# Stage 4 of a decoder kernel: the order of one pair's work on TensorE, and score matmuls of 512 columns

## The reference

```python
q = x @ Wq                                    # x: 32 x 64 x 128
xc = jnp.concatenate((mem, x), axis=1)        # mem: the context, so 128 keys
k, v = jnp.split(xc @ Wkv, 2, axis=-1)        # 16 heads of depth 8
dots = jnp.einsum('bhid,bhjd->bhij', q, k) * scale
dots = jnp.where(j_idx > i_idx + mem_len, -jnp.inf, dots)   # causal over the own tokens
attn = jax.nn.softmax(dots, axis=-1)
out = jnp.einsum('bhij,bhjd->bhid', attn, v).transpose(0, 2, 1, 3).reshape(b, n, dim)
return out @ Wout + bout                      # then x = layernorm(x + out)
```

## Time and profile before

| | before |
|---|---|
| median of 3 runs | 856.89 us (855.67 to 860.06) |
| the profiled execution, its own time | 857.85 us |
| its span, first to last instruction | 856.0 us |
| TensorE busy | 770.1 us, 90% |
| weight loads | 389.4 us, 45% |
| VectorE busy | 493.0 us, 58% |
| ScalarE busy | 405.6 us, 47% |
| mean granted TensorE clock | 0.971 of 2.4 GHz |
| chain that ended last, by engine | PE 68%, VectorE 15%, issue 8%, ScalarE 7% |
| stage 4, from its first scores to its last output projection | 535.1 to 678.6 us |

### The profile page before, as it was taken

The page is one execution under the profiler, slowest core; times in us unless marked ns, Lnnn a source line. Parts: engine busy times, 40 slices in busy tenths (PEclk is TensorE's granted clock), DMA queues, the critical chain, the costliest instruction groups (busy, mean ns, idle before and its releaser), DMA issues.

```text
span 856.0 us, 17678 instructions
## 1 busy us (share of the span) xinstructions
PE 770.1 (90%) x6937; PEld 389.4 (45%) x6937; DVE 493.0 (58%) x1166; ACT 405.6 (47%) x735; POOL 111.0 (13%) x107
## 2 busy tenths in 40 slices
PE   6999999999789977999995877989898799999996
PEld 4435344445455543334332555455565443443332
DVE  1553232234788876765746786566665576646662
ACT  2726455473566663234244233456554444553454
POOL 1271121212000000000003345221120000000000
PEclk9999999999899998999997898999999999999998
DMA  9400000000000000000000000000000000000000
GB/s 360 179 2 1 1 0 0 1 2 1 1 2 2 0 3 0 0 2 0 0 0 1 1 1 0 2 3 4 3 4 3 2 1 0 2 0 1 12 13 26
DMA packets 2375, 13.56 MB, mean 16 GB/s; under 512 B 256, under 2 KB 256, under 8 KB 1664
## 3 DMA queue, kind: packets, MB, share of 16 engines
q1 hardware_dynamic: 2304, 12.56, 3.7%
HBM read 11.51 MB, written 1.05 MB: 15 GB/s over the span
## 4 chain that ended last, share of the span: by engine, by line
PE 68%; DVE 15%; issue 8%; ACT 7%; DMA 1%; DVEq 0%; POOL 0%; ACTq 0%; SPq 0%
PE bank L1737 6%; PE bank L2356 4%; PE bank L1963 3%; PE bank L2282 3%; PE bank L1775 3%; PE bank L2335 3%; PE bank L2292 3%; PE bank L1788 3%; PE bank L1979 3%; PE bank L2115 3%; PE bank L1968 3%; PE bank L2176 2%; PE bank L121 2%; DVE sb_rowmax L1105 2%; PE bank L2180 2%
## 5 line engine op out<-in xcount | busy, mean ns | idle before, releaser
L1737 PE MATMUL bank<-sb_xT,sb_arena 128*128 128x512 f32 (+1 forms) x128 | 65.2, 644 | 3.5 <-ACT sb_arena L608 2.5
L1424 DVE TENSOR_REDUCE sb_rowmax<-bank 128x4 f32<-128x512 f32 x64 | 41.2, 685 | 30.0 <-PE bank L2137 30.0
L608 ACT ACTIVATE sb_arena<-bank 128x512 f32<-128x512 f32 x64 | 37.4, 597 | 39.3 <-PE bank L1737 39.3
L1036 DVE TENSOR_TENSOR sb_arena<-bank,sb_arena 128x512 f32<-128x512 f32 x32 | 22.1, 690 | 50.2 <-PE bank L1788 49.9
L760 ACT ACTIVATE sb_arena<-bank 128x512 f32<-128x512 f32 x36 | 21.4, 596 | 55.7 <-PE bank L1963 54.1
L517 POOL TENSOR_TENSOR sb_arena<-sb_la,sb_consts 128x1024 f32<-128x1024 f32 x16 | 30.5, 1919 | 114.3 <-PE bank L1775 90.3
L855 ACT ACTIVATE sb_arena<-bank 128x512 f32<-128x512 f32 x64 | 33.0, 603 | 22.4 <-PE bank L2146 22.4
L1737 PEld LDWEIGHTS bank<-sb_xT,sb_arena 128*128 128x128 f32 x128 | 23.3, 200 | 38.4 <-ACT sb_arena L608 21.8
L1963 PE MATMUL bank<-sb_xT,sb_w 128*128 128x512 f32 (+1 forms) x72 | 40.7, 648 | 0.0
L2115 PE MATMUL bank<-sb_arena 32*64 32x256 f32 x512 | 35.1, 387 | 4.0 <-issue 2.2
L1657 DVE TENSOR_TENSOR sb_arena<-sb_arena,bank 128x512 f32<-128x512 f32 x32 | 21.0, 684 | 29.7 <-PE bank L2339 22.0
(11 more groups left out here) (352 smaller groups left out, 1692.7 us busy)
## 6 DMA issues: line engine op xcount, KB each, us to landing
sb_w<-w SPq DMA_DIRECT2D x1, 2646.5 KB, 26.7
sb_consts<-consts SPq DMA_DIRECT2D x1, 1812.0 KB, 13.4
sb_w<-w SPq DMA_DIRECT2D x1, 1736.0 KB, 19.3
sb_w<-w SPq DMA_DIRECT2D x1, 1175.0 KB, 8.3
sb_arena<-w SPq DMA_DIRECT2D x2, 512.0 KB, 4.3
sb_ctxT<-ctx SPq DMA_DIRECT2D x1, 1024.0 KB, 15.4
out<-sb_xT SPq DMA_DIRECT2D x4, 256.0 KB, 2.4
sb_xT<-x SPq DMA_DIRECT2D x1, 768.0 KB, 9.7
```

Of the source, the lines that this page charges most:

```text
L608: act.activation(V[:, h, :], bank[h % 2][:], ACT.Copy).then_inc(s_vev, 1)
L1424: dve.tensor_reduce(rowmax4[k % 2][:, 4 * g:4 * g + 4], bank[n][:].rearrange("p (j t) -> p j t", j=4), AX, ALU.max).then_inc(s_mx4, 1)
L1737: pe.matmul(bank[h % 2][:], KT[:, h, :], cols(c), start=True, stop=True).then_inc(s_v, 1)
```

## The change

Four things are changed, all in stage 4.

1. The order within one i on TensorE. It is now: first half of the scores, `turn4(i-1)`, `pv4(i-2)`, second half, `less_max4(i-1)`, projection, tail. The transpose of a pair's maxima thus moves from the end of its own i to the next one, and the projections from between the halves to the end.
2. The scores by query: 4 matmuls of 512 columns instead of 8 of 256 in each call. The 8 by key stay, but stand behind them in one run instead of alternating with them.
3. VectorE and ScalarE follow: VectorE divides pair i-2 (and scales a chunk) between the two maxima; ScalarE takes the first two exponentials of a pair, then copies keys or values, then takes the other two; the copy of the maxima stands at the head of i.
4. The tables of the tail move two places ahead (the last entries stay), some waits are counted anew, and the second query projection goes to bank 7 like the later ones.

```diff
-    projected_q4 = [bank[6], bank[5]] + [bank[7]] * (2 * NCH - 2)
+    projected_q4 = [bank[6]] + [bank[7]] * (2 * NCH - 1)
-    OUT_AT, VAR_AT4 = {7: 0, 11: 1, 15: 2}, {9: 0, 13: 1, 16: 2}
-    SCALE_AT4, LOGITS_AT = {10: 0, 14: 1, 16: 2}, {12: 0, 15: 1, 17: 2}
+    OUT_AT, VAR_AT4 = {5: 0, 9: 1, 13: 2}, {7: 0, 11: 1, 15: 2}
+    SCALE_AT4, LOGITS_AT = {8: 0, 12: 1, 16: 2}, {10: 0, 14: 1, 17: 2}
...
 # ScalarE, stage4
+                if 1 <= i <= PAIRS:
+                    maxima_copy4(i - 1)
+                    exps4(i - 1, 0)
                 if i % 2 == 0 and h < HALVES:
                     k_copy4(h)
                 if i % 2 and h < HALVES:
                     v_by_head4(h)
+                if 1 <= i <= PAIRS:
+                    exps4(i - 1, 1)
...
-                if 1 <= i <= PAIRS:
-                    exps4(i - 1)
-                if i < PAIRS:
-                    maxima_copy4(i)
                 if i % 2 == 0 and h < HALVES:
                     k_by_head4(h)
...
 # VectorE, stage4, behind maxima4(i, 0)
+                if i >= 2:
+                    divided4(i - 2)
+                if i == 2:
+                    hook(1)
+                if i in SCALE_AT4:
+                    tail4(SCALE_AT4[i], 1)
+                if i < PAIRS:
+                    maxima4(i, 1)
+                    split4(i)
                 if i % 2 == 0 and i // 2 + 1 < HALVES:
                     q_copy4(i // 2 + 1)
...
 # TensorE, k_project4 and v_project4
-            wait(pe, s_o4, 2 * h - 4)
+            wait(pe, s_o4, 2 * h - 3)
-            wait(pe, s_o4, 2 * h - 1)
+            wait(pe, s_o4, 2 * h)
...
 # TensorE, scores4
-            for part in range(2):
-                at = slice(SEQ * part, SEQ * part + SEQ)
-                if k < PAIRS:
-                    for g in groups:
-                        scored = bank[g % 2][:].rearrange("p (j t) -> p j t", j=4)
-                        for b in range(2):
-                            q = (b0 + b) * SEQ
-                            pe.matmul(scored[64 * b:64 * b + 64, :, at], q4[rows(g), q:q + SEQ], kx4[rows(g), b0 + b, :, at],
-                                      start=(part == 0), stop=True, skip_group_check=(part == 1))
-                if k > 0:
+            if k < PAIRS:
+                for g in groups:
+                    for b in range(2):
+                        q = (b0 + b) * SEQ
+                        pe.matmul(bank[g % 2][64 * b:64 * b + 64, :], q4[rows(g), q:q + SEQ],
+                                  kx4[rows(g), b0 + b].rearrange("p j t -> p (j t)"), start=True, stop=True)
+            if k > 0:
+                for b in range(2):
                     for g in key_groups:
                         for h in range(2):
...
 # TensorE, stage4, behind scores4(i, 0)
+                if 1 <= i <= PAIRS:
+                    turn4(i - 1)
+                if i >= 2:
...
+                    pv4(i - 2)
+                else:
+                    keep_warm(6)
+                if i <= PAIRS:
+                    scores4(i, 1)
+                if 1 <= i <= PAIRS:
+                    less_max4(i - 1)
                 if i % 2 == 0 and i // 2 + 1 < HALVES:
                     k_project4(i // 2 + 1)
```

More of the change, by code:

```diff
@@ L849, in v_by_head4, with exps4 @@
                                ACT.Copy).then_inc(s_vx4, 1)
-        def exps4(k):
+        def exps4(k, pair):
             wait(act, s_pv4, k - 1)
-            for n, g in enumerate(KEY_GROUPS):
+            for n in (2 * pair, 2 * pair + 1):
+                g = KEY_GROUPS[n]
                 wait(act, s_t4, 4 * k + n + 1)
@@ L2120, in scores4 @@
                             o = slice(64 * h, 64 * h + 64)
-                            pe.matmul(by_key[g][o, 256 * part:256 * part + 256], k4[(k - 1) // 2 % 3][rows(g), e0 + part, o],
-                                      qx4[rows(g), 2 * ((k - 1) % 4) + part].rearrange("p j q -> p (j q)"),
-                                      start=(part == 0), stop=True, skip_group_check=(part == 1))
+                            pe.matmul(by_key[g][o, 256 * b:256 * b + 256], k4[(k - 1) // 2 % 3][rows(g), e0 + b, o],
+                                      qx4[rows(g), 2 * ((k - 1) % 4) + b].rearrange("p j q -> p (j q)"),
+                                      start=(b == 0), stop=True, skip_group_check=(b == 1))
             if k > 0:
@@ L2210, in stage4 @@
                 if i == 0:
-                    wait(pe, s_qc4, 1)
+                    wait(pe, s_resid, 4 * NCH)
                 if i in LOGITS_AT:
@@ L2221, in stage4 @@
                     tail4(VAR_AT4[i], 2)
-                if i == 0:
-                    keep_warm(6)
-                if i <= PAIRS:
-                    scores4(i, 1)
-                if 1 <= i <= PAIRS:
-                    less_max4(i - 1)
-                if i >= 2:
-                    if i % 2 == 0:
-                        wait(pe, s_kx4, 5 * min(i // 2 + 1, HALVES - 1) + 1)
-                    else:
-                        wait(pe, s_vx4, min(4 * (i // 2) + 4, 4 * HALVES))
-                    pv4(i - 2)
-                if i == 0:
-                    keep_warm(6)
-                if i < PAIRS:
-                    turn4(i)
             return lambda part: tail4(NCH - 1, part)
@@ L2244, in tail4 @@
                 wait(pe, s_lnv, t)
-                wait(pe, s_zt, c if c > 1 else 0)
+                wait(pe, s_zt, NCH - 1 if is_last(c) else 0)
                 pe.matmul(bank[7][:], w(4, "wo"), attn4[c % 2], start=True, stop=True).then_inc(s_po4, 1)
```

14 lines of the change are left out of this document (5 added, 9 removed).

## The result

| | before | changed |
|---|---|---|
| median | 857.31 us (853.64 to 862.94, 6 runs) | 847.47 us (844.96 to 849.52, 6 runs) |
| ratio to before | | 0.9881, 95% interval 0.9842 to 0.992 |
| span of the profiled execution | 856.0 us | 845.5 us |
| mean granted clock | 0.971 | 0.975 |
| stage 4, first scores to last output projection | 143.5 us | 133.8 us |

The kernel is faster by 1.2% (0.8 to 1.6%). The forecast was 846 us, in a range of 840.5 to 854, so it held.

What follows compares the result with a forecast made beforehand. TensorE was taken to set the pace in stage 4, so only its idle time could be won: opening 3.8, middle 0.6 + 2.6, end 3.8, in sum 11.0, giving 846.9 for the profiled execution and 846 as median; range 840.5 to 854.

Steps and rivals of the forecast that it cites:

- Opening: Start of stage 4: i = 3 starts at 557.8 instead of 561.64, the transpose's 1.55 wait and low clock gone; 3.8 won.
- bare order: i = 3 to 13 without pauses: the new order takes 79.0 us against 79.6, scaling delays included; 0.6 won.
- 2.6 for pauses: i = 3 to 13: TensorE runs out of instructions less often; 2.6 won, between bounds of 0 and 7.6.
- the scaling: VectorE at i = 8 and 12: ahead of the second half's maxima it delays the next first half, 1.0 lost twice.
- The step "about 0.16": The time counted for the transpose on TensorE in each i, about 0.16 us.
- The reading of the 1.80 between the halves: Old order: two row maxima of VectorE set the 1.80; projections fill 1.48 or 1.0, so TensorE idles 0.3 or 0.8.
- 512 columns: Scores by query: by-key passes go on beside the longer ones, a half's scores stay at 0.86; cost 0.
- second rival: Scores: long passes hold back short ones; 6.4 us more (852.4) or 12.8 more (858.8); chance 0.16.
- the third: Scores: by-key work runs only when by-query work has ended, 0.86 more a half, 25.8 in all: 872; chance 0.05.
- End: From i = 14 on: 26.0 instead of 29.8, 3.8 won; waits for maxima (1.81) and behind logits (2.21) go.
- No low clock in stage 4: Sign of a right forecast: the new timeline shows no low clock anywhere in stage 4.
- the fourth rival: ScalarE's exponentials bind: pv4 waits 0.3 to 0.4 in 13 i, 4.5 us in all, so 850.5; chance 0.08.

Runs made afterwards that it cites:

- 128-column kernel: The changed kernel with its scores by query in 16 matmuls of 128 columns instead of 4 of 512: 853.32 us, 0.9928 of the kernel before.
- order-only kernel: The changed kernel with part 2 undone, its scores by query again in 8 matmuls of 256 columns: 843.38 us, 0.9825 of the kernel before.
- transpose late: The changed kernel with turn4(i-1) moved behind pv4(i-2) instead of ahead of it: 846.67 us, 0.9863 of the kernel before.

## Why the prediction was right, and where not

**Opening**, 3.8 forecast, 3.35 measured. The wait of the transpose and the low clock behind it went as told. What was missed: at i = 2 the transpose starts 0.68 behind the masks, not 0.33, as it waits for the logarithm of stage 3's last chunk (0.28 of wait at 550.2).

**Middle**, 0.6 for the bare order and 2.6 for pauses, 3.2 in sum; measured 2.7. The sum is near, its parts are less so. Counted alike in both traces, the pauses between i = 3 and 13 went from 6.8 to 3.2 us (1.84, 0.76 and 0.60), 3.6 less. Then without them the middle takes 84.48 - 3.20 = 81.3 us against 87.20 - 6.76 = 80.4 before: the bare order, forecast to win 0.6, lost 0.8. Counted by the phases that hold the pauses (their length less the 1.90 of an undisturbed `pv4`, 1.05 of scores and 0.34 of `less_max4`) the pauses cost 7.7 before and 3.8 after, and the bare order lost 1.2. So its sign is sure, its size is not. The terms of it that were right: the wait at i = 3 (0.46, forecast 0.5), and the scaling (0.82 twice, forecast 1.0 twice). The term that was left out: the transpose shares bank 7 with the variance, and waits for ScalarE at i = 8 and 12, 0.4 each. The step "about 0.16" took the transpose's cost from a place where nothing of the tail stood near it, though the tables moved the variance to the end of the i just ahead of it. This 0.8 is a good half of what was missed; no run tells what the rest is. The reading of the 1.80 between the halves left something out too: at even i the idle 0.3 lies ahead of the projection, which waits there for VectorE's L1410, as its row says. The maxima run behind the same copies and end at 603.84, so that the 1.80 holds.

**Pauses.** The reading of the earlier trace rows as want of instructions is borne out by the 128-column kernel and by the place of the pauses in the count of records. The reason given for the amount is not. The 2.6 rested on 8% fewer instructions and on what stands ahead of `pv4`. The order-only kernel has the 8% back and fewer pauses (2.5 against 5.1), and a shift of 128 instructions moves them by 6.6 us. That the estimate came near was luck in part: with 128 instructions put ahead of stage 4, the same change is at 851.77 us, 4 us slower by the medians and 2.6 by the ratios, whose intervals overlap (still inside the range). The prediction named the range of this term, 0 to all of it, but not the thing that decides within it.

**512 columns**, forecast at 0. In the matmuls it is 0: a half with masks is 1.38 us as before, with by-key passes of 256 columns going beside by-query passes of 512. That rules out the second rival (long passes hold back short ones, 1.6 or more a half) and the third (serialised). Its order of starts is again against the rule of strict program order in "TensorE: Matmul & The Clock Gate" of the Trainium skill, Part 3, What overlaps and what doesn't: L2121 starts 0.03 behind L2114, and the second passes of L2114, which stand ahead of it in the program, start at 596.30, when L2121's first ones are done.

**End**, 3.8 forecast, 3.6 measured. The 1.81 and the 2.21 of before are gone. In their place stand a pause of 1.64 in the chain's third row (1.0 was allowed for all pauses there) and a low clock from 663.1 on. "No low clock in stage 4" was wrong: that TensorE waits there for the last exponentials and for the division was in the forecast's sum, and the earlier trace rows show what can follow a wait.

**ScalarE's chain**, the fourth rival, does not bind: no `pv4` waits for exponentials from i = 3 to 13. **The sum**, 11.0, stands against 9.7 in stage 4 and 10.5 in the span; 0.8 of those 10.5 lie where the change does nothing (2.6 ahead of stage 4, less 1.8 behind it). By the medians it is 857.31 - 847.47 = 9.8.

## What to carry to other kernels

Where the bound engine is fed with small instructions, look in the timeline for gaps with no releaser amid work that waits for nothing, and count the records between them, those of waits included. If they lie at multiples of 256, a comparison of two kernels also compares where the borders of their blocks fall; here that alone was worth up to 8 us of 850. Before crediting such a difference to an edit, pad the program ahead of it by 64 and 128 instructions and time both kernels again. And when a piece of work is moved, list who writes to its bank near the new place: here the program makes the transpose wait until the variance in its bank has been read.

## What the runs showed of the hardware

- TensorE's pauses without a releaser lie at multiples of 256 of its records, and those of over 0.5 us end 2.2 to 2.9 us after a packet of 16 KB on the instruction queue has begun. They take 0.3 to 1.9 us, behind blocks with 2.6 to 7.0 us of work; at other borders between blocks of such lengths there is none. The same border had a pause of 1.84, 1.70 and 0.27 us in three executions (of kernels that are alike up to there), and its packet had begun 2.42, 2.30 and 1.01 us behind the border before.
- 64 tiny matmuls inside a wait of stage 3 cost the order-only kernel 8.1 us, 6.2 of them in stage 4 of the profiled execution.
- Passes of 512 and of 256 columns in different rows of the array go on side by side: a half's scores take 1.05 us with by-query matmuls of 256 or of 512 columns, and with 16 matmuls of 128 it is 1.09 (594.40 to 595.49) where no pause falls in it.
- In the changed kernel the clock stood at its lower level for 6.8 us from 663.1 on. Ahead of that TensorE had been idle for 0.51 and 0.71 us around logits of 8 columns, and it waited 1.43 us more meanwhile. In the order-only kernel's trace, with the same waits and no warm-up matmuls either, it did not fall. Of nine such traces five show it, of three with warm-up matmuls in these waits none. In one trace (transpose late) it fell in the middle of stage 4, behind a pause of 1.86 us, and L2083 took 2.08 us instead of 1.12.

What stays open: what decides when a packet begins, and why it begins at different times for the same border. No run told these apart.
